# Three attention stages of a decoder kernel rewritten from grouped steps into straight beats

## The reference, cut to what matters

```python
q = jnp.einsum('bsc,hcd->bhsd', xn, wq)
k = jnp.einsum('btc,hcd->bhtd', yn, wk)
v = jnp.einsum('btc,hcd->bhtd', yn, wv)
a = jax.nn.softmax(jnp.einsum('bhsd,bhtd->bhst', q, k) * D ** (-0.5), axis=-1)
if causal:
    a = a * mask
o = jnp.einsum('bhst,bhtd->bhsd', a, v)
x_out = x + o @ li1_w + li1_b
```

## Time and profile before

| | us |
|---|---|
| median of 3 runs | 4159.24 |
| lowest and highest | 4155.75, 4160.47 |
| the profiled execution's own time | 4173.35 |
| span in its trace | 4171.5 |

### The profile page before, as it was taken

One profiled execution on the slowest core, in us unless ns is written; L12 is line 12 of the kernel. 1 busy time (PEld: TensorE's weight loads), 2 busy tenths in 40 slices (PEclk: granted clock), 3 DMA queues, 4 the chain that ended last, 5 costly groups with the idle time before them and its releaser, 6 DMA issues. The chain is left out here.

```text
span 4171.5 us, 104540 instructions
## 1 busy us (share of the span) xinstructions
PE 3456.3 (83%) x41696; PEld 2257.9 (54%) x41696; DVE 2515.9 (60%) x5780; ACT 1949.0 (47%) x3810; POOL 2008.4 (48%) x1742
## 2 busy tenths in 40 slices
PE   7898889886888888777999979778888688888576
PEld 3444444443455555554666657645555455556476
DVE  6877877785656565474555548656666543433265
ACT  5555555552444444333555544245555344443154
POOL 5666766664567676561111116346666300102455
PEclk8999999997999999897999989879999788885598
DMA  3211212114600000000000000000000000000286
GB/s 117 77 74 76 76 68 77 70 74 156 218 2 2 2 2 2 15 15 4 5 5 5 4 10 1 10 1 0 0 0 0 10 5 6 5 4 14 76 260 194
DMA packets 48939, 181.24 MB, mean 43 GB/s; under 512 B 11678, under 2 KB 23073, under 8 KB 39360
## 3 DMA queue, kind: packets, MB, share of 16 engines
q1 hardware_dynamic: 44224, 167.68, 12.0%
q0 software_dynamic: 4352, 8.47, 0.6%
HBM read 167.13 MB, written 43.65 MB: 51 GB/s over the span
## 5 line engine op out<-in xcount | busy, mean ns | idle before, releaser
L494 DVE TENSOR_TENSOR_SCAN XC<-ssm_dA,ssm_db 128x2048 f32<-128x2048 f32 x128 | 565.6, 4419 | 148.3 <-PE ssm_db L349 124.7
L556 POOL TENSOR_TENSOR XC<-XC,XB 128x1536 f32<-128x1536 f32 x128 | 493.5, 3856 | 297.9 <-DVE XC L494 165.9
L363 PE MATMUL ssm_y<-XC,ssm_wt 128*128 128x512 f32 x1024 | 495.5, 629 | 1.6 <-POOL XC L556 1.6
L438 ACT ACTIVATE ssm_dA<-ssm_delta,ssm_nega 128x508 f32<-128x508 f32 x512 | 325.0, 707 | 107.3 <-DVE XC L494 107.3
L1138 POOL TENSOR_TENSOR self_pm<-self_pT,self_wt 128x512 f32<-128x512 f32 x256 | 320.9, 1291 | 68.7 <-ACT self_pT L912 68.7
L363 PEld LDWEIGHTS ssm_y<-XC,ssm_wt 128*128 128x128 f32 x1024 | 197.0, 200 | 230.8 <-issue 221.5
L2326 POOL TENSOR_TENSOR XC<-XC,gla_wt 128x512 f32<-128x512 f32 x128 | 160.7, 1276 | 159.5 <-ACT XC L2177 159.5
L1149 POOL TENSOR_TENSOR XC<-XC,XB 128x128 f32<-128x128 f32 x128 | 58.9, 460 | 363.9 <-DVE XB L1055 363.9
L349 PE MATMUL ssm_db<-XB,ssm_dxT 32*128 32x128 f32 x4096 | 175.4, 300 | 69.5 <-DVE XC L494 67.8
L126 POOL TENSOR_SCALAR narrow_rstd<-narrow_mv 128x4 f32<-128x4 f32 x16 | 3.6, 228 | 458.6 <-DVE narrow_mv L121 458.6
L349 PEld LDWEIGHTS ssm_db<-XB,ssm_dxT 32*128 32x128 f32 x4096 | 146.3, 199 | 135.0 <-DVE XC L494 110.9
(11 more groups left out here) (431 smaller groups left out, 8934.0 us busy)
## 6 DMA issues: line engine op xcount, KB each, us to landing
XB<-c_rows SPq DMA_DIRECT2D x64, 1024.0 KB, 4.5
experts_we<-in_w_experts SPq DMA_DIRECT2D x72, 579.0 KB
sorted<-in_padding SPq DMA_DIRECT2D x1, 33280.0 KB
experts_rt<-sorted SPq DMA_DIRECT2D x72, 65.0 KB
ssm_xT<-in_xT SPq DMA_DIRECT2D x16, 256.0 KB, 4.6
self_wt<-in_w_self SPq DMA_DIRECT2D x1, 1412.0 KB, 6.1
mlp_wt<-in_w_mlp SPq DMA_DIRECT2D x1, 1347.0 KB, 5.9
cross_ctx_t<-in_ctx SPq DMA_DIRECT2D x16, 77.0 KB
```

Of the source, the lines that this page charges most:

```text
L363: mm = pe.matmul(yp[half][:, :].rearrange("p (b t) -> p b t", b=GROUP), ident, of_state(states(32, at), k), start=False, stop=(nq == 3 and ...
L438: o = act.activation(dA[:, p % 2, :].rearrange("p (b k t) -> p b k t", b=GROUP, k=4)[:, :, k, 1:T], by_batch(delta[:, slot, half, :])[:, : ...
L494: dve.tensor_tensor_scan(states(0, p).rearrange("p m t -> p (m t)"), dA[:, p % 2, :], db[:, :], 0.0, ALU.mult, ALU.add).then_inc(h_ready, 1)
L556: pool.tensor_tensor(states(32, p).rearrange("p (b k) t -> p b k t", k=4)[:, :, 0:3, :], states(0, p).rearrange("p (b k) t -> p b k t", k= ...
```

## The change

The loops `step`, `lagged`, `run` and the table `places` go. In their place every engine runs one straight loop over beats t, from -1 to the end, with a fixed list of calls. Between S2 and the next S1 stand project, the "early" jobs and sums; between S1 and the next S2 stand PV, turn and the "late" jobs. On DVE the maxima now stand ahead of `oT`, and the norms stand ahead of the maxima and serve the group after next. On ACT exp comes first, then inverse, jobs and turned; on POOL the mask comes first. S2 waits for the maxima bank by bank. In the narrow stage S1 is cut into two halves of two banks each, with a wait and a semaphore step for each half, and x is transposed straight from X, without POOL's copy. Only the jobs of `FRONT` run ahead of the first beat: in self attention the four v jobs no longer stand there, in cross attention neither of the two.

```diff
         if own:
             jobs = [("x", 0, "act")] + [("q", j, "act") for j in range(NT)] + [("k", j, "act") for j in range(NT)]
             jobs += [("v", b, "dve") for b in range(GROUP)]
-            places = [(1, 1)] + [(2, 0)] * 3 + [(2, 1)] * 3 + [(3, 0)] * 3 + [(3, 1)] * 3
+            late = {0: (0,), 1: (1, 2, 3, 4), 2: (5, 6, 7, 8), 3: (9, 10)}
+            early = {3: (), 4: (11, 12)}
         else:
             jobs = [("x", 0, "act"), ("c", 0, "act")] + [("q", j, "act") for j in range(NT)]
             jobs += [("k three", 0, "act"), ("k", NT - 1, "dve")] + [("v", b, "dve") for b in range(2)]
-            places = [(1, 1)] * 2 + [(2, 0)] * 2 + [(2, 1)] * 2 + [(3, 0), (3, 1), (4, 0), (4, 1)]
+            late = {0: (0, 1), 1: (2, 3, 4, 5), 2: (6,), 3: (8,)}
+            early = {3: (7,), 4: (9,)}
...
+        def early_jobs(t):
+
+            g, p = t // GROUP, t % GROUP
+            found = [(g + 1, n) for n in early.get(p, ())] + [(g, n) for n in early.get(p + GROUP, ())]
+            return [(k, n) for k, n in found if 0 <= k < NG]
...
+        def late_jobs(t):
+
+
+            g, p = t // GROUP, t % GROUP
+            return [(g + 1, n) for n in late[p] if g + 1 < NG]
+
+        FIRST = [n for p in range(3) for n in late[p]] + ([] if own else [7])
+        FRONT = [(0, n) for n in sorted(FIRST)]
 
...
-            def first_scores(n, b, s):
+            job = job_own if own else job_context
+
+            def first_scores(n):
+                s, b = n // GROUP % 2, n % GROUP
+                if b == 0:
+                    pe.wait_ge(by_act, (n // GROUP + 1) * N_ACT)
+                    if not own:
+                        pe.wait_ge(by_dve, n // GROUP * N_DVE + K_DVE)
+                if n >= 3:
+                    pe.wait_ge(exp_ready, 4 * (n - 2))
+                elif n:
+                    pe.wait_ge(max_ready, 4 * n)
                 for j in range(NT):
                     for r in range(4):
...
                     for r in range(4):
+                        if j == 0:
+                            pe.wait_ge(max_ready, 4 * (min(n + 3, N) - 1) + r + 1)
+                            if n + 3 > N:
+                                pe.wait_ge(exp_ready, 4 * (n - 1) + r + 1)
                         rows = slice(32 * r, 32 * r + 32)
-                        pe.matmul(sc[r][0:TK, j * T:(j + 1) * T], pick[rows, j, 0:TK], nmT[rows, b % 2, :],
...
+            for g, n in FRONT:
+                job(g, n)
+            for t in BEATS:
+                if there(t - 2):
+                    second_scores(t - 2)
+                if there(t - 4):
+                    project(t - 4)
+                for g, n in early_jobs(t):
+                    if (g, n) not in FRONT:
+                        job(g, n)
+                if there(t - 3):
+                    sums(t - 3)
+                if there(t + 1):
+                    first_scores(t + 1)
+                if there(t - 3):
+                    weighted(t - 3)
+                if there(t):
+                    turn(t)
+                for g, n in late_jobs(t):
+                    job(g, n)
 
         @block.scalar
...
+            for t in BEATS:
+                if there(t - 2):
+                    probabilities(t - 2)
+                if there(t - 3):
+                    inverse(t - 3)
+                if there(t):
+                    turned(t)
+                for g, n in late_jobs(t):
+                    empty(g, n)
 
...
+            def norms(t):
+                g, p = t // GROUP + 2, t % GROUP
+                if g < NG:
+                    if own and p == 0:
+                        x1_stats(g)
+                    if own and p == 1:
+                        x1_norm(g)
+                    if p == 2:
+                        in_stats(g)
+                    if p == 3:
+                        in_norm(g)
...
+            for t in BEATS:
+                if there(t):
+                    split(t)
+                if there(t - 4):
+                    add(t - 4)
+                for g, n in early_jobs(t):
+                    if (g, n) not in FRONT:
+                        empty(g, n)
+                norms(t)
+                if there(t + 1):
+                    maxima(t + 1)
+                if there(t - 3):
+                    scaled(t - 3)
+                for g, n in late_jobs(t):
+                    empty(g, n)
 
...
+            for t in BEATS:
+                if own and there(t - 2):
+                    masked(t - 2)
+                if there(t - 4):
+                    advance(t - 4)
+                norms(t)
...
+            def first_scores(n):
+                s, b = n // GROUP % 2, n % GROUP
+                if b == 0:
+                    pe.wait_ge(by_act, (n // GROUP + 1) * N_ACT)
+                for two in range(2):
+                    if n >= 3:
+                        pe.wait_ge(exp_ready, 4 * (n - 3) + 2 * two + 2)
+                    elif n:
+                        pe.wait_ge(max_ready, 4 * (n - 1) + 2 * two + 2)
+                    for j in range(4):
+                        for r in (2 * two, 2 * two + 1):
                             rows = slice(32 * r, 32 * r + 32)
-                            mm = pe.matmul(sc[r][0:TK, :].rearrange("p (j t) -> p j t", j=4),
-                                           kT[rows, s, b * TK:(b + 1) * TK], qm[rows, s, :, b * T:(b + 1) * T],
...
+            for t in BEATS:
+                if there(t - 2):
+                    second_scores(t - 2)
+                if there(t - 4):
+                    project(t - 4)
+                if g := comes(t, 0):
+                    turn_x(g)
+                if g := comes(t, 1):
+                    queries(g)
+                if g := comes(t, 2):
+                    context(g)
+                if there(t - 3):
+                    sums(t - 3)
+                if there(t + 1):
+                    first_scores(t + 1)
+                if there(t - 3):
+                    weighted(t - 3)
+                if there(t):
+                    turn(t)
...
+            def maxima(n):
+                if n:
+                    dve.wait_ge(split_ready, 2 * n)
+                for r in range(4):
+                    dve.wait_ge(s1_mm, 2 * n + r // 2 + 1)
+                    dve.tensor_reduce(nmax[:, r, :], sc[r][:, 0:4 * TK].rearrange("p (h t) -> p h t", h=4),
+                                      AX.X, ALU.max, negate=True).then_inc(max_ready, 1)
...
+            for t in BEATS:
+                if there(t):
+                    split(t)
+                if g := comes(t, 3):
+                    values(g)
+                if there(t - 4):
+                    add(t - 4)
+                if there(t + 1):
+                    maxima(t + 1)
+                if there(t - 3):
+                    scaled(t - 3)
+                if t % GROUP == 0 and there(t - 8):
+                    measure(t // GROUP - 2)
+                if t % GROUP == 1 and there(t - 9):
+                    norm(t // GROUP - 2)
 
         @block.gpsimd
```

More of the change, by code:

```diff
@@ L673, in k_cols @@
             return slice(2 * TK * (j % 3), 2 * TK * (j % 3) + 2 * TK)
-        def run(eng, head, step):
-            head(0, 0, None, None)
-            step(0, 0, range(GROUP))
-            for g in range(1, NG + 1):
-                step(g, g % 2, range(GROUP))
-        def there(g, ahead):
-            return not isinstance(g, int) or g + ahead < NG
-        def late(g):
-            return 0 < g < NG
-        def lagged(g, p, lag, slot):
-            n = g * GROUP + (p - lag)
-            if isinstance(n, int) and not 0 <= n < N:
-                return None
-            return n, (g if p >= lag else g - 1), (p - lag) % GROUP, slot if p >= lag else 1 - slot
         @block.sync
@@ new lines, in project @@
+            def project(n):
+                pe.wait_ge(oT_ready, n + 1)
+                for j in range(NT):
+                    mm = pe.matmul(ob[:, 0:C], oT[:, j, :], wo[:, j * C:(j + 1) * C], start=(j == 0), stop=(j == NT - 1))
+                mm.then_inc(out_mm, 1)
+            for g, n in FRONT:
[18 more added lines that the diff above has]
+                    job(g, n)
@@ L942, in _, with inverse @@
-            run(act, head, step)
+                    act.activation(pT[0:TK, n % 2, r, :], sc[r][0:TK, :], ACT.Exp).then_inc(exp_ready, 1)
+            def inverse(n):
+                act.wait_ge(sum_mm, n + 1)
+                if n:
+                    act.wait_ge(oT_ready, n)
+                act.activation(rinv[:, :], sb[:, :], ACT.Ln).then_inc(ln_ready, 1)
+                act.wait_ge(ln_ready, n + 1)
+                act.activation(rinv[:, :], rinv[:, :], ACT.Exp, scale=-1.0).then_inc(rinv_ready, 1)
@@ new lines, in sums @@
+            def sums(n):
+                pe.wait_ge(exp_ready, 4 * n + 4)
+                pe.wait_ge(nmT_ready, min(n + 3, N))
+                if n:
+                    pe.wait_ge(ln_ready, n)
+                for j in range(4):
```

(20 more changed lines are left out.)

852 lines of the change are left out of this document (339 added, 513 removed).

## The result

The changed kernel took 3961.09 us (median of four runs, 3958.64 to 3962.75) and the kernel before 4159.85: ratio 0.9525, 95% interval 0.9506 to 0.9544, 199 us less. One of the four runs of the kernel before took 5071 in a slow state and does not enter the ratio. The prediction was 4020 in a range of 3935 to 4105: the direction was right, and the gain was put 60 us too low. The profiled execution took 3961.34, with a span of 3959.3 against 4171.5.

The account below looks back on a forecast made before the run. PE was taken as near its limit in cross, with self's maxima delayed behind `oT` and narrow's clock low; 31 + 4 + 17 + 2 + 83, plus 1 for a POOL copy, is 138: 4173 to 4035, less 14, said 4020 (3935 to 4105).

Parts of the forecast that it names:

- Self, 31 + 4: Self attention: beats of 9.1 and three of 9.9, group 38.8 against 40.74, saves 31 us; four v jobs leaving the front, 4.
- the norms that wait out four masks: Self, beat p=3: each of four DVE norm instructions waits out one POOL mask, putting the beat 2.3 us over, at 9.9.
- `oT` ahead of the maxima as the cost of before: Self and cross, DVE: `oT` waits for ACT's `rinv`, 207 us in self, and so delays the maxima listed behind it.
- Cross, 17 + 2: Cross attention: group of 31.9 against 33.07 saves 17 us; two v jobs fewer at the front save 2.
- Narrow, 83: Narrow attention: group of 23.1 against 28.21 at full clock; with an assumed share of low clock, a gain of 83 us.
- the ring: Attention's four score banks, maxima to S2 to exp to next maxima: 7.6 us self, 6.5 cross, 5.1 narrow after the change.
- 20% of the time at 1.2 GHz: Narrow: assumed share of low clock after the change, giving a mean beat of 6.3 us and 397 us for 63 beats.
- The rule of the Trainium skill that I cited and weighed low: Narrow: the clock gate starts throttled and activity opens it, so a denser stage gets more clock, a gain of 103 us.
- 1 (more, 3970): Whole kernel: norms not held under masks (30 us more), narrow's clock rises to cross's (20 more): 3970; chance 0.25.
- 2: Less gain: narrow's clock stays, and q bursts or a late `oT` hold PE, project standing first behind S2: 4100; chance 0.21.
- 3: Slower: self and cross fall to narrow's clock, 36% of the time at 1.2 GHz: 4244; chance 0.08.
- 4: No effect: ring and job places don't limit; groups stay 40.7, 33.1 and 28.2: 4159, give or take 8; chance 0.04.

Follow-up runs that it names:

- wide alone: The kernel before with self and cross attention in the new straight beats and narrow left as it was: 4057.8 us, ratio 0.9794 to the kernel before.

## Why the prediction was right, and where it was short

*Self, 31 + 4.* The mechanism was right, the total in part by luck. The four beats came within 0.25 of the forecast, the norms that wait out four masks among them, now shown by two experiments. The group fell by 2.2, not 1.9, which makes 35; 27.4 are left. The beats of before took 7.7 less than 15.75 full groups, because the first and the last are shorter. Those of the changed kernel took as much as 15.75 groups, because about every other group has a piece at the low clock and takes 40.1 instead of 38.5 (the granted clock is 0.97 for 0.98). The tail gave 3.4 that I had at zero, and so 34 stand beside the 35.

*`oT` ahead of the maxima as the cost of before.* Right as one half: without that swap the rest of the change loses 13 us in self and 20 in cross. But with nothing but the swap self loses 205, where I expected 36. What `oT`'s place cost before, by itself, no run can tell.

*Cross, 17 + 2.* This step was mis-sized: it is 49. The mechanism held: the beats came within 0.3, the group at 31.35 for 31.9, and this is 9 of the 30 missed. 11 lie in the step from group to stage. I multiplied by 15.75 groups for both kernels; but the beats of before took 4 more than 15.75 groups and those of the changed kernel 6 less. Most of that is the clock, 0.98 for 0.96 (four groups of before took 36.0 to 36.3 instead of 33.1, none of the changed kernel behind its first did), part that the last beats carry no jobs, 6.45 us each for the last two, 7.08 and 7.07 before. The front gave 6.6: there two v jobs took 4.3 (1905.33 to 1909.67), 1.09 for the first, 1.3 of waiting for its bank and 1.99 for the second at the low clock, where I had 2 for both at full clock; and a norm no longer runs beside POOL's spread (1.11 for 2.05). The tail gave 5.1.

*Narrow, 83.* Right by two errors that cancel. The beats were put at 23.1 a group and are 24.56, 23 us too little: I took half of S1 out of the ring, but not that S1 in halves is longer, 1.64 in place of the 1.13 of the kernel before:

```profile
3572.05 1.13 PE L1306 MATMUL narrow_scores<-narrow_kT,narrow_qm 32*128 32x77 f32 x32 [0.38 <-ACT narrow_pT L1404]
```

A half of S1 has only two of the four strips of 32 rows to take turns in; PE then bounds three of the four beats. With S1 whole again in the changed order it takes 1.13, so it is the cut and not the place. That products in different strips of rows overlap is what the Trainium skill says in "TensorE: Matmul & The Clock Gate", "Part 3: Packing small matmuls — row/col tiling"; the trace agrees, the same 32 records in 1.64 with two strips and in 1.13 with four. Against it stood the clock: I took 20% of the time at 1.2 GHz, 33 us, and it is 2.4 us over 15.75 groups. Of the 91 us in the beats 57 are the ring and 33 the clock. The rule of the Trainium skill that I cited and weighed low ("TensorE: Matmul & The Clock Gate", "What's actually happening"), by which activity opens the gate, fits this trace: 0.82 before, 0.96 with PE hardly ever idle. The tail gave 10.5, at 0.96 where it was at 0.50; the old tail took 19.8 in the one profile that had it at 0.94 (wide alone), so some 8 of the 10.5 are clock and 2 the order.

*The rivals.* 1 (more, 3970) was nearest in time (3961), and half right in its reasons: narrow's clock did rise, but the norms were held up. 2: no S2 waited for `oT` or POOL, but its thought is what the swap alone met: project stands in front of S1's work. 3: no, both stages kept 0.97 and 0.98. 4: no, each stage's groups changed.

*Not foreseen at all:* tails, 19 us together, some 8 of them the clock of narrow's, and the experts stage, some 20 us that are not the change's. What stays open is why the tail of narrow is at either clock, why experts differs between jobs by some 20 to 27 us, and what beside idle time sets the clock; no run here separates that.

## What to carry to other kernels

Find what stands ahead of the ring's own instructions in each engine's list; move it behind, and move the other engine's order with it, since either half alone was slower than nothing (self 906 or 714 against 701). Price an edit by the whole stage, front and tail included, and where PE idles at a lowered clock count the clock as a possible gain of its own: it was 33 of the 91 us in narrow's beats. If a helper of two SBUF inputs or a tensor_scalar must run beside a busy POOL, put it where nothing waits for it.

## What the runs showed of the hardware

- More products made a stage faster: with three extra of 128 columns a beat narrow's clock was 0.94 instead of 0.80, its span 493.7 instead of 514.9 to 533.2, and the whole kernel 26 us shorter.
- A stage can be at a low clock though PE never waits long. PE's own waits in narrow before, at 0.82, us in total, times, longest:

```profile
PE narrow_scores L1333 <- DVE narrow_nmax L1462: 53.3, 45, 1.8
PE narrow_scores L1306 <- ACT narrow_pT L1404: 27.3, 36, 3.5
```

- A PE that counts as busy can stay slow: in experts it is busy for 20.00 of 20 us and granted 0.50 (the kernel before, profiled again; the same for 70 us on two chips, on the third for the stage's first 20):

```profile
3846.00:3866.00 20.00, 20.00 (x97) 20.00 (x98) 9.42 (x51) 7.04 (x19) 15.12 (x17) 0.50 0.16 52
```

- Four norms of 128x128 take 1.11 with POOL idle (the front of cross), 1.75 beside one POOL instruction, and 4.62 under four.
